# Two one-hot blocks in an expert layer, unread products in TensorE's waits, and three small edits in a quantised layer

## The chip, the cores and the metric

The kernel runs on one core of a Trainium2 chip. The metric is the time of one execution on the device in microseconds. Engines are named as the profile names them: PE (TensorE), PEld (its weight loads), DVE (VectorE), ACT (ScalarE), POOL (GpSimd), SP (SyncE, which issues most transfers).

## The reference

The input is x of 4 x 16 x 16 x 192 in f32: 1024 tokens of 192 numbers. Six layers follow one another, each added to its input; the change touches the last four.

```python
x = x + scan(_gn(x))            # state-space scan, four directions
x = x + neighbour(_gn(x))       # 7x7 neighbourhood attention
t = _to_tokens(x)
t = t + quantised(_ln_t(t))     # int8 attention and MLP
t = t + expert_m(_ln_t(t))      # 16 experts, top 2, and a shared one
t = t + attention(_ln_t(t))     # plain attention, one head
t = t + expert_g(_ln_t(t))      # 8 experts, top 2
```

The quantised layer rounds at every step: `fq(x, s) = clip(round(x / s), -128, 127) * s`.

```python
x_norm = fq(layernorm(x, g1, beta1), s_n1)
qkv = fq(x_norm @ fq(w_qkv).T + b_qkv, s_qkv)       # 12 heads of 16
attn = int_softmax(fq(q @ k.T * scale, s_attn))     # integer exponent, 2^(30-q)
x_attn = fq((attn @ v) @ fq(w_proj).T + b_proj, s_sv)
x = fq(x + x_attn, s_r1)
x_norm = fq(layernorm(x, g2, beta2), s_n2)
h = fq(gelu(x_norm @ fq(w_fc1).T + b_fc1), s_act)
h = fq(h @ fq(w_fc2).T + b_fc2, s_m2)
x = fq(x + h, s_r2)
```

The first expert layer:

```python
scores = softmax(xf @ gate_w.T)                     # 1024 x 16
topw, topi = top_k(scores, 2)
h = silu(xf @ w1[e].T) * (xf @ w3[e].T) * comb      # 512 wide, for the tokens of expert e
y = h @ w2[e].T ; z = silu(xf @ sw1.T) * (xf @ sw3.T) @ sw2.T
```

## The kernel before

Each layer is a block of its own; all engines finish one before the next begins. PE's time by layer: quantised 383 to 630 us, expert layer m 630 to 895, attention 895 to 960, last layer g 960 to 1104.

**Quantised layer** (`quantised_layer`). Tokens lie as 8 tiles of 128 (`X[:, t, :]`). The start normalises them (DVE), turns them on PE (f32 transposes, L1679), clips them on DVE into `nT` (bf16) and multiplies by `wqk` (`project`, L1696). Then 48 steps follow, one for each pair of image and head (4 images of 256 tokens, 12 heads). A head's chain is: PE scores (L1722), ACT rounds into `lt` (L1590), POOL clips (L1241), DVE takes the maximum (L1420) and subtracts it (`xi`, two L1425), POOL makes the quotient `qi` (L1251) and the power of two `e2` (L1268, 16-bit integers whose bits are read as bf16), PE forms the remainder in PSUM (L1742, L1743), ACT squares it (L1604), DVE multiplies by `e2` with a running sum (two L1443). `e2` has two buffers: before L1268 POOL waits until DVE is through with head h-2. Later PE turns the weights (L1734), DVE copies them (L1433), and the values are weighted. Each step of DVE's loop (index n) also carries side work: U of the first normalisation (L1476, tile n-12 for n = 12 to 19), the rescaled bias rows at n = 22 (L1478 to L1486), and after every image its `requantise`, on POOL for images 0 to 2 (L1214 to L1236).

The tail after the last head: DVE requantises image 3 (L1502 to L1507), statistics and N (L1362 to L1375), PE turns N (`turn_norm`, L1785), DVE clips into `nT` (L1389, L1391), PE makes 12 `up_product`s (L1823, two matmuls each: FT = 6 tiles for each half of the tokens), ACT the gelu (L1660), DVE rounds and clips it into `hi` (L1531, L1520, L1526), PE makes 4 `down_product`s. Each of these handles two token tiles, and begins a tile's sum with the bias row: `ones` (1 x 128) times `brow` (1 x 192), both f32 (L1837), then 6 bf16 matmuls (L1839). ACT evicts (L1667), DVE and ACT end the layer (L1544 to L1554, L1617).

**Expert layer m** (`expert_layer`, gated). After the normalisation `U` is split in f16 parts (`U16` is the high and the low part), PE turns it (L2429) and makes the logits, DVE picks two experts for each token and gives each token its places (slots) in the experts' lists. The plan is a list of blocks of 256 tokens: four shared blocks (0 to 3) and 23 routed ones. A block is `up_block` (40 matmuls, L2489 to L2493), silu on ACT (L2398), product with the gate on DVE (L2182), its high part on ACT (early blocks, L2413) or POOL (L2105), its low part on DVE (L2193), and `down_block` (L2511 to L2513). POOL writes all tokens to their slots in `scratch_x` in HBM by 16 indirect transfers (L2117); SP then reads each routed block's rows back (`load_rows`), after the last of the 16. PE turns the rows (six L2464) and ACT copies them into `xt` (L2375). Outputs go through `scratch_y` and are combined at the end. The layer g has the same form and already fetches its first three blocks by one-hot matmuls (`DIRECT` = 3): DVE compares a row of slot numbers with each token's seat (L2806), and PE multiplies the tokens with it.

Weights of a block come as f32 and are split by ACT (L2334, L2335, L2343) and DVE (L2167, L2169, L2175); `lo_ab` tells PE that a set's up weights are there. SP loads a set when DVE has left its stage.

Of the kernel before, what the change touches and what calls it, by code (L numbers as in the profile page):

```python
# [25 lines left out]
NB = 4  # L26
# [1096 lines left out]
def quantised_layer(nc, K, X, D):  # L1123

    with ExitStack() as stack:
# [25 lines left out]
        e2 = ctx.sb("q_e2", [P, 2, QT, L], I16)  # L1151
# [13 lines left out]
        brow = ctx.sb("q_brow", [1, C])  # L1165
        ones = ctx.sb("q_ones", [1, P])
# [9 lines left out]
        taken, late_part = S("taken"), S("late_part")  # L1176
# [23 lines left out]
        with nc.Block() as block:  # L1200
# [7 lines left out]
            def _(pool):  # L1208
                def requantise(at, p, part):
# [7 lines left out]
                    elif part == 1:  # L1217
                        pool.wait_ge(pool_steps, at + 2)
                        pool.tensor_scalar(f, f, -MAGIC, sc[:, S_SV:S_SV + 1], ALU.add, ALU.mult).then_inc(pool_steps, 1)
                        pool.wait_ge(pool_steps, at + 3)  # L1220
                        pool.tensor_tensor(f, f, batch(U, p), ALU.add).then_inc(pool_steps, 1)
# [37 lines left out]
                for h in range(HEADS):  # L1259
# [6 lines left out]
                    if h >= 2:  # L1266
                        pool.wait_ge(expd, (h - 1) * QT)
                    pool.tensor_scalar(e2[:, h % 2, :, :].rearrange("p q k -> p (q k)"), qi[:, h % 2, :], -128.0,  # L1268
                                       (127 + EXP_N + CENTRE) * 128.0, ALU.mult, ALU.add).then_inc(expo, 1)
                    if h % HG == HG - 1 and h < HEADS - NH:  # L1270
                        pool.wait_ge(scores, h + 1)
                        take(h // NH + 1, h % NH // HG)
                    if h >= TURN + 4 and h < TURN + 4 + 2 * NH and (h - TURN - 4) % NH < 3:
# [10 lines left out]
            def _(v):  # L1284
# [151 lines left out]
                def exponential(e):  # L1436
# [5 lines left out]
                    for q in range(QT):  # L1442
                        v.scalar_tensor_tensor(ex[:, e % NH, q, :], ps[:, 5 + e % 2, q * L:(q + 1) * L], k(K_CI), e2[:, e % 2, q, :].bitcast(BF16),  # L1443
# [17 lines left out]
                for n in range(STEPS):  # L1461
# [12 lines left out]
                    if 12 <= n < 12 + NT:  # L1474
                        t = n - 12
                        step(v.tensor_scalar(U[:, t, :], X[:, t, :], mv[:, t, 0:1], rs[:, 0, t:t + 1], ALU.subtract, ALU.mult))  # L1476
                    if n == 22:
# [7 lines left out]
                        step(v.tensor_scalar(brow[:, :], rows[0:1, 2, :], kf[0:1, K_PER:K_PER + 1], None, ALU.mult))  # L1485
# [24 lines left out]
                v.wait_ge(proj_read, 4)  # L1510
                requantise(3, S_SV, S_R1)
# [162 lines left out]
            def _(pe):  # L1674
                for half in range(NHALF):
# [7 lines left out]
                pe.wait_ge(K["q"]["quantised"], 20)  # L1683
# [24 lines left out]
                for n in range(6):  # L1708
                    project(n)
                pe.wait_ge(constants, 1)  # L1710
# [80 lines left out]
                for n in range(STEPS):  # L1791
# [1643 lines left out]
```

## Time and profile before

| | us |
|---|---|
| three runs, median | 1108.9 |
| three runs, lowest and highest | 1105.35 and 1115.82 |
| the profiled execution's own time | 1105.46 |
| its span on the core | 1103.7 |
| mean granted clock of PE in it | 0.817 of full speed |

The page shows the busy time of each engine and, in 40 slices, the clock that PE was granted. A stretch of the trace gives the same by windows. A timeline lists instructions in order with the idle time before them and what ended it. A group adds up all instructions of one line and shape. A "clock" of 1.00 is 2.4 GHz, of 0.50 it is 1.2 GHz; a number between is a stretch that holds both.

### The profile page before, as it was taken

What the parts mean: (1) busy time and instruction counts of PE and PEld (TensorE: products, weight loads), DVE (VectorE), ACT (ScalarE), POOL (GpSimd) and SP (SyncE); (2) the same over time, 40 slices, a digit from 0 to 9 for tenths busy, and PEclk for the clock granted to TensorE, in tenths of its full rate; (3) what the DMA queues carried; (4) which work ended last, traced back from release to release, by engine and by line L of the source; (5) the groups of instructions that cost most, each with busy time, mean ns of one, the idle gap of its engine ahead of it and who ended that gap; (6) DMA issues with size and microseconds to landing.
All of it is one profiled execution on the core that took longest, in us unless ns stands there. A gap on an engine that the chain in (4) does not pass through costs nothing. (4 is left out here: it accounts for less than half of the span.)

```text
span 1103.7 us, 17587 instructions
## 1 busy us (share of the span) xinstructions
PE 871.8 (79%) x6053; PEld 587.6 (53%) x6053; DVE 802.4 (73%) x1699; ACT 578.8 (52%) x977; POOL 424.3 (38%) x458
## 2 busy tenths in 40 slices
PE   8779999985999746667775564999999838658991
PEld 3333333333579722223452354999888715557991
DVE  6589999994675379998976673788888475583763
ACT  2755454421466445776764342677776146256760
POOL 0016666644046337668750005222222520034335
PEclk8889999996999865555556567999999958869996
DMA  8176666503000000000000093699994455102653
GB/s 254 42 205 171 170 168 161 152 20 86 1 2 2 11 2 1 1 1 1 1 1 1 13 230 100 166 269 267 257 270 126 136 155 154 52 26 84 209 206 89
DMA packets 61592, 117.59 MB, mean 107 GB/s; under 512 B 10240, under 2 KB 37312, under 8 KB 61504
## 3 DMA queue, kind: packets, MB, share of 16 engines
q1 hardware_dynamic: 58432, 110.18, 36.0%
q0 software_dynamic: 3072, 6.30, 1.9%
q8 instruction: 48, 0.79, 0.3%
q14 instruction: 40, 0.33, 0.1%
HBM read 90.79 MB, written 16.81 MB: 97 GB/s over the span
## 5 line engine op out<-in xcount | busy, mean ns | idle before, releaser
L459 POOL TENSOR_TENSOR hC<-hs,Cb 128x1024 f32<-128x1024 f32 x47 | 110.8, 2358 | 125.8 <-DVE hs L498 125.8
L498 DVE TENSOR_TENSOR_SCAN hs<-ps_l,dBu 128x1024 f32<-128x1024 f32 x48 | 109.9, 2290 | 2.8 <-ACT ps_l L590 1.2
L2105 POOL CAST m_h_hi<-m_h 128x512 f16<-128x512 f32 x54 | 49.0, 907 | 137.5 <-DVE m_h L2182 137.5
L658 PE MATMUL ps_l<-hC,selT 128*96 128x512 f32 x192 | 93.2, 609 | 1.5 <-POOL hC L459 1.5
L643 PE MATMUL ps_l<-du,sel 96*128 96x512 f32 x192 | 90.5, 593 | 1.4 <-DVE dBu L491 1.4
L590 ACT ACTIVATE ps_l<-d_sp,Am 128x1020 f32<-128x1020 f32 x48 | 53.5, 1115 | 71.5 <-DVE hs L498 71.3
L2511 PE MATMUL ps_m<-m_wd_hi,m_h_hi 128*128 128x192 f16 x248 | 62.9, 254 | 6.6 <-issue 3.5
L1742 PE MATMUL ps_l<-q_xi,identh 128*128 128x512 f16 x48 | 28.8, 599 | 48.5 <-POOL q_qi L1251 24.8
L2193 DVE TENSOR_TENSOR m_h_lo<-m_h,m_h_hi 128x512 f16<-128x512 f32 x62 | 42.9, 693 | 33.2 <-POOL m_h_hi L2105 30.1
L782 POOL TENSOR_TENSOR n_Pl<-n_PT,n_Ph 128x352 f16<-128x352 f32 x48 | 40.8, 853 | 65.6 <-ACT n_Ph L910 48.3
L2398 ACT ACTIVATE m_act<-ps_m 128x512 f32<-128x512 f32 x62 | 36.8, 593 | 52.8 <-PE ps_m L2493 48.6
L491 DVE TENSOR_TENSOR dBu<-ps_l,Bb 128x512 f32<-128x512 f32 x96 | 60.7, 674 | 4.0 <-PE ps_l L643 3.9
L2512 PE MATMUL ps_m<-m_wd_lo,m_h_hi 128*128 128x192 f16 x248 | 63.0, 254 | 0.0
L2513 PE MATMUL ps_m<-m_wd_hi,m_h_lo 128*128 128x192 f16 x248 | 63.0, 254 | 0.0
L643 PEld LDWEIGHTS ps_l<-du,sel 96*128 96x128 f32 x192 | 34.3, 188 | 51.2 <-DVE dBu L491 37.0
L658 PEld LDWEIGHTS ps_l<-hC,selT 128*96 128x96 f32 x192 | 27.4, 162 | 58.8 <-POOL hC L459 31.9
L2749 POOL DMA_INDIRECT scratch_x<-g_U,g_slot x16 | 19.3, 1208 | 96.9 <-DVE g_who L2867 89.8
L1599 ACT ACTIVATE q_pi<-q_ex,q_kf,q_fac 128x256 f16<-128x256 f32 x96 | 51.4, 589 | 0.8 <-PE ps_l L1734 0.8
L2489 PE MATMUL ps_m<-m_xt,m_wa_hi 128*128 128x256 f16 x184 | 50.4, 274 | 1.1
L2117 POOL DMA_INDIRECT scratch_x<-m_U,m_slot x16 | 17.3, 1080 | 87.4 <-DVE m_who L2276 77.9
L2182 DVE SCALAR_TENSOR_TENSOR m_h<-ps_m,m_act 128x512 f32<-128x512 f32 x62 | 42.5, 685 | 11.5 <-ACT m_act L2398 6.5
L2492 PE MATMUL ps_m<-m_xt,m_wb_hi 128*128 128x256 f16 x184 | 50.2, 273 | 0.0
(576 smaller groups left out, 2894.0 us busy)
## 6 DMA issues: line engine op xcount, KB each, us to landing
d_sp<-scan_d SPq DMA_DIRECT2D x48, 512.0 KB, 4.4
m_sta<-in_m_ua SPq DMA_DIRECT2D x25, 512.0 KB, 4.3
m_stb<-in_m_ub SPq DMA_DIRECT2D x50, 256.0 KB, 5.8
m_std<-in_m_dn SPq DMA_DIRECT2D x25, 384.0 KB, 6.7
gw_dn_in<-gw_dn SPq DMA_DIRECT2D x10, 576.0 KB, 3.3
scratch_x<-zero SPq DMA_DIRECT2D x1, 4416.0 KB, 21.1
m_xg<-scratch_x SPq DMA_DIRECT2D x23, 192.0 KB, 6.4
scratch_y<-m_o SPq DMA_DIRECT2D x23, 192.0 KB, 6.5
```

The source lines that it names most:

```text
L459: pool.tensor_tensor(hC[:, n % 2, :], hs[:, n % 2, :], Cb[:, which(n), :], ALU.mult).then_inc(weighted, 1)
L491: v.tensor_tensor(dBu[:, n % 2, half * BANK:(half + 1) * BANK], ps[:, 4 + half, :], Bb[:, which(n), half * BANK:(half + 1) * BANK], ALU.mu ...
L498: v.tensor_tensor_scan(hs[:, n % 2, ::step], dA(n)[:, ::step], dBu[:, n % 2, ::step], 0.0, ALU.mult, ALU.add).then_inc(scanned, 1)
L590: act.activation(dst[:, :, o:o + L - 1], d_sp[:, n % NSP, :].rearrange("p (b t) -> p b t", t=L)[:, :, o:o + L - 1], ACT.Exp, scale=Am[:, c ...
L643: pe.matmul(ps[:, 4 + half, :], sel[:, n % NG, :], du[:, n // NG, half * BANK:(half + 1) * BANK], start=True, stop=True).then_inc(du_bc, 1)
L658: mm = pe.matmul(ps[0:DI, 6 + half, :], selT[:, n % NG, :], hC[:, n % 2, half * BANK:(half + 1) * BANK], start=(n == STEPS), stop=(m == ST ...
L1599: act.activation(pi[:, p % 2, q, :], ex[:, p % NH, q, :], ACT.Identity, scale=fac[:, p % NH, q:q + 1], bias=kf[:, K_FLOOR:K_FLOOR + 1]).th ...
L2489: pe.matmul(out, wa_hi[a][:, col], x[:, 0, :], start=True, stop=False)
L2492: pe.matmul(out, wb_hi[a][:, col], x[:, 2, :], start=False, stop=False)
L2511: pe.matmul(out, h_hi[:, b % 2, f // 2, tok], wd_hi[a][:, col], start=(f == 0), stop=False)
L2512: pe.matmul(out, h_hi[:, b % 2, f // 2, tok], wd_lo[a][:, col], start=False, stop=False)
L2513: mm = pe.matmul(out, h_lo[:, b % 2, f // 2, tok], wd_hi[a][:, col], start=False, stop=(f == tiles - 1))
```

## The change

1. **Unread products.** `keep_busy(pe, K, out, n)` issues n matmuls of 96 rows by 512 columns in bf16 into a PSUM bank that nothing reads before it is written again. It stands at nine places: quantised layer, at the start (18; the wait for the quantised weights moves ahead of it), behind the first six `project` (14, behind a wait for `n_ready` 4), behind the last head's `shifted` (7), ahead of `turn_norm(6, 8)` (10, behind a wait for `proj_read`), ahead of `up_product(FT)` (10) and ahead of the last two `down_product` (5, behind a wait for all gelus); at the start of expert layer m (15), of the attention (11) and of the last layer (15).
2. **Quantised layer.** `e2` gets a third buffer. The eight U operations move from DVE (n = 12 to 19) to POOL (h = 12 to 19), with a negated mean `nmean` made by DVE at n = 11; waits `minus` and `unit` guard them. The bias row becomes three bf16 parts in three rows, `ones` three rows in bf16: DVE makes 9 small operations where there was one, PE one bf16 matmul of three rows where it had one f32 matmul of one row.
3. **Expert layer m.** `DIRECT` is 2: routed blocks 0 and 1 (plan blocks 4 and 5) take their tokens by one-hot matmuls (24 of 256 columns each) in place of reading rows from `scratch_x` and six transposes. DVE makes `seat` and the one-hot matrices, eight L2806-like operations of 128 x 256 for each block, in plan blocks 1 and 2. ACT makes the high parts for six blocks instead of four (`EARLY`). The first read of rows is for plan block 6.

```diff
+def keep_busy(pe, K, out, n):
+    w = K["q"]["wqk"]
+    for _ in range(n):
+        pe.matmul(out, w[:, 0:P], w[:, 0:BANK], start=True, stop=True)
...
-        e2 = ctx.sb("q_e2", [P, 2, QT, L], I16)
+        e2 = ctx.sb("q_e2", [P, 3, QT, L], I16)
...
-        brow = ctx.sb("q_brow", [1, C])
-        ones = ctx.sb("q_ones", [1, P])
+        brow = ctx.sb("q_brow", [3, C], BF16)
+        brest = ctx.sb("q_brest", [3, C])
+        bpart = ctx.sb("q_bpart", [3, 3, C], BF16)
+        nmean = ctx.sb("q_nmean", [P, NT])
+        ones = ctx.sb("q_ones", [3, P], BF16)
...
+                        pool.wait_ge(unit, NT)
                         pool.tensor_tensor(f, f, batch(U, p), ALU.add).then_inc(pool_steps, 1)
...
-                    if h >= 2:
-                        pool.wait_ge(expd, (h - 1) * QT)
-                    pool.tensor_scalar(e2[:, h % 2, :, :].rearrange("p q k -> p (q k)"), qi[:, h % 2, :], -128.0,
+                    if h >= 3:
+                        pool.wait_ge(expd, (h - 2) * QT)
+                    pool.tensor_scalar(e2[:, h % 3, :, :].rearrange("p q k -> p (q k)"), qi[:, h % 2, :], -128.0,
...
+                    if 12 <= h < 12 + NT:
+                        t = h - 12
+                        pool.wait_ge(minus, 1)
+                        pool.tensor_scalar(U[:, t, :], X[:, t, :], nmean[:, t:t + 1], rs[:, 0, t:t + 1], ALU.add, ALU.mult).then_inc(unit, 1)
...
-                    if 12 <= n < 12 + NT:
-                        t = n - 12
-                        step(v.tensor_scalar(U[:, t, :], X[:, t, :], mv[:, t, 0:1], rs[:, 0, t:t + 1], ALU.subtract, ALU.mult))
+                    if n == 11:
+                        v.tensor_scalar(nmean[:, :], mv[:, :, 0], -1.0, None, ALU.mult).then_inc(minus, 1)
...
-                        step(v.tensor_scalar(brow[:, :], rows[0:1, 2, :], kf[0:1, K_PER:K_PER + 1], None, ALU.mult))
+                        step(v.tensor_scalar(brest[:, :], rows[0:3, 2, :], kf[0:3, K_PER:K_PER + 1], None, ALU.mult))
+                        for part in range(3):
+                            step(v.tensor_copy(bpart[:, part, :], brest[:, :]))
+                            if part < 2:
+                                step(v.tensor_tensor(brest[:, :], brest[:, :], bpart[:, part, :], ALU.subtract))
+                        mine = lambda part: K["ident"][0:3, part:part + 1]
+                        step(v.tensor_scalar(brow[:, :], bpart[:, 0, :], mine(0), None, ALU.mult))
+                        for part in (1, 2):
+                            step(v.scalar_tensor_tensor(brow[:, :], bpart[:, part, :], mine(part), brow[:, :], ALU.mult, ALU.add))
...
+                pe.wait_ge(K["q"]["quantised"], 20)
+                keep_busy(pe, K, ps[:, 0, :], 18)
...
+                pe.wait_ge(n_ready, 4)
+                keep_busy(pe, K, ps[:, 4, :], 14)
                 pe.wait_ge(constants, 1)
...
+                pe.wait_ge(shifted, HEADS)
+                keep_busy(pe, K, ps[:, 0, :], 7)
                 turn_sums(NB - 1)
...
+                pe.wait_ge(proj_read, NB)
+                keep_busy(pe, K, ps[:, 7, :], 10)
                 turn_norm(6, 8)
-                for n in range(4, FF2 - 2):
+                for n in range(4, FT):
+                    up_product(n)
+                keep_busy(pe, K, ps[:, 7, :], 10)
+                for n in range(FT, FF2 - 2):
                     up_product(n)
                 for p in range(2):
                     down_product(p)
                     up_product(FF2 - 2 + p)
+                pe.wait_ge(gelu, FF2)
+                keep_busy(pe, K, ps[:, 0, :], 5)
                 for p in (2, 3):
                     down_product(p)
...
-    DIRECT = 0 if gated else 3
-    EARLY = (FIRST if gated else DIRECT) * PAIRS
+    DIRECT = 2 if gated else 3
+    EARLY = (FIRST + DIRECT) * PAIRS
...
+                step(v.scalar_tensor_tensor(seat[:], rank, 1.0, both[:], ALU.add, ALU.mult))
                 if not gated:
-                    step(v.scalar_tensor_tensor(seat[:], rank, 1.0, both[:], ALU.add, ALU.mult))
                     one_hot(0)
...
+                    if gated and 1 <= b <= DIRECT:
+                        one_hot(b - 1)
...
             def _(pe):
+                keep_busy(pe, K, ps[:, 7, :], 15)
```

The last line stands in expert layer m and in the last layer; the attention has the same with 11. What `one_hot` and `turn` do in the one-hot case:

```python
for t in range(NT):      # DVE, one_hot(n)
    v.tensor_scalar(hot[:, n % 2, t, :], slots1[:, :], seat[:, t, n:n + 1], None, ALU.is_equal)
for part in range(PARTS_X):      # PE, turn(b): PARTS_X = 3, NT = 8
    for t in range(NT):
        pe.matmul(out, U16[:, t, part * P:(part + 1) * P], hot[:, n % 2, t, :], start=(t == 0), stop=(t == NT - 1))
```

## Rows read from the trace of the kernel before

**Rows 1.** The page: PE's granted clock in 40 slices of the span (27.6 us each)

```profile
PEclk8889999996999865555556567999999958869996
```

**Rows 2.** Stretches (from:to, length, busy us of PE, PEld, DVE, ACT, POOL; clock, DMA, GB/s)

```profile
389.30:392.70 3.40, 2.94 (x14) 2.77 (x15) 3.12 (x15) 1.11 (x2) 0.00 (x0) 0.50 0.00 0
...
392.80:396.20 3.40, 2.05 (x11) 0.90 (x10) 3.08 (x15) 2.67 (x5) 0.00 (x0) 1.00 0.01 2
...
480.00:565.00 85.00, 61.90 (x333) 30.55 (x333) 79.03 (x245) 61.24 (x108) 61.92 (x98) 0.50 0.00 1
...
600.70:614.40 13.70, 13.31 (x44) 6.54 (x44) 6.64 (x21) 3.88 (x5) 0.00 (x0) 0.50 0.00 0
...
614.40:630.20 15.80, 8.14 (x33) 4.92 (x32) 12.02 (x30) 5.84 (x9) 0.00 (x0) 0.50 0.00 1
...
645.50:673.80 28.30, 25.09 (x224) 21.83 (x224) 20.21 (x69) 11.96 (x18) 9.27 (x8) 0.88 0.67 172
...
673.80:688.50 14.70, 0.02 (x1) 0.00 (x0) 2.08 (x3) 1.85 (x3) 8.02 (x9) 0.58 0.27 87
...
695.40:842.00 146.60, 145.58 (x1505) 132.59 (x1504) 121.58 (x150) 104.63 (x150) 39.62 (x42) 1.00 0.93 252
```

**Rows 3.** Groups of DVE, 400 to 572 us (count | busy, mean ns | idle before, releaser)

```profile
L1420 DVE TENSOR_REDUCE q_nm<-q_lt 128x2 f32<-128x512 f16 x48 | 32.6, 679 | 6.8 <-POOL q_lt L1241 6.3
...
L1476 DVE TENSOR_SCALAR q_U<-X,q_mv,q_rs 128x192 f32<-128x192 f32 x8 | 3.1, 393 | 0.0
...
L1485 DVE TENSOR_SCALAR q_brow<-q_rows,q_kf 1x192 f32<-1x192 f32 x1 | 0.3, 307 | 0.0
```

**Rows 4.** All 96 instructions of line 1425 by duration

```profile
L1425 DVE TENSOR_SCALAR q_xi<-q_lt,q_nm,q_kf x96: 333/394/778, 407.0 to 562.3; 128x256 f16<-128x256 f16 x96
```

**Rows 5.** Groups of POOL, 400 to 572 us

```profile
L1268 POOL TENSOR_SCALAR q_e<-q_qi 128x512 int16<-128x512 f16 x48 | 29.7, 618 | 12.4 <-DVE q_ex L1443 10.4
...
L1231 POOL TENSOR_SCALAR q_U<-q_pj,q_sc 128x384 f32<-128x384 f32 x2 | 1.2, 581 | 0.2
```

**Rows 6.** Timeline of PE at the quantised layer's start and tail, DVE's last rows

```profile
394.50 2.87 PE L1696 MATMUL ps_l<-q_nT,q_wqk 96*128 96x512 bf16 x12 [1.35 <-DVE q_nT L1330]
...
600.68 3.59 PE L1823 MATMUL ps_l<-q_nT,q_w 96*128 96x512 bf16 x8 [4.34 <-DVE q_nT L1391]
...
604.67 0.97 PE L1837 MATMUL ps_l<-q_brow,q_ones 1*128 1x192 f32 x2 [0.39 <-DVE q_hi L1526]
...
605.58 1.14 PE L1839 MATMUL ps_l<-q_w,q_hi 128*128 128x192 bf16 x6
...
629.63 0.56 DVE L1554 TENSOR_TENSOR X<-X,q_pj 128x384 f32<-128x384 f32 x1
```

**Rows 7.** Expert layer m: timelines of POOL, PE, DVE and ACT; SyncE's wait, 695 to 842

```profile
637.57 2.74 PE L2429 MATMUL ps_m<-identh,m_U 128*128 128x128 f16 x24 [12.36 <-ACT m_U L2353]
...
677.58 0.60 ACT L2398 ACTIVATE m_act<-ps_m 128x512 f32<-128x512 f32 x1 [2.41 <-DMA beta<-in_out_b]
...
683.52 0.96 POOL L2117 DMA_INDIRECT scratch_x<-m_U,m_slot  x1 [0.36 <-DMA scratch_x<-m_U,m_slot]
...
688.51 0.82 PE L2464 MATMUL ps_m<-identh,m_xg 128*128 128x128 f16 x6 [14.70 <-DMA m_xg<-scratch_x]
...
694.29 1.22 DVE L2167 SCALAR_TENSOR_TENSOR m_wa_lo<-m_sta,m_wa_hi 128x1024 f16<-128x1024 f32 x1
...
701.23 1.22 DVE L2167 SCALAR_TENSOR_TENSOR m_wa_lo<-m_sta,m_wa_hi 128x1024 f16<-128x1024 f32 x1
...
708.90 0.59 ACT L2398 ACTIVATE m_act<-ps_m 128x512 f32<-128x512 f32 x1
...
SPq L2032 <- DVE m_wd_lo L2175: 67.5, 19, 10.8
```

**Rows 8.** Last layer, group of DVE: its own one-hot instruction

```profile
L2806 DVE TENSOR_SCALAR g_hot<-g_slots,g_seat 128x128 f16<-128x128 f16 x48 | 8.6, 272 | 0.0
```

**Rows 9.** Timeline of PE at the start of the attention

```profile
899.19 3.88 PE L1866 MATMUL ps_l<-ident,a_U 128*96 128x128 f32 x16 [16.84 <-DVE a_U L178]
```

More of the change, by code:

```diff
@@ L1175, in quantised_layer @@
             S("proj"), S("evac"), S("q_part"), S("qk_ready"), S("v_proj"), S("v_steps"), S("v_ready"))
-        taken, late_part = S("taken"), S("late_part")
+        taken, late_part, minus, unit = S("taken"), S("late_part"), S("minus"), S("unit")
         scores, shifted, clipped, negmax, diff, quot, rest, expo, square, expd, factor = (
@@ L1442, in exponential @@
                     for q in range(QT):
-                        v.scalar_tensor_tensor(ex[:, e % NH, q, :], ps[:, 5 + e % 2, q * L:(q + 1) * L], k(K_CI), e2[:, e % 2, q, :].bitcast(BF16),
+                        v.scalar_tensor_tensor(ex[:, e % NH, q, :], ps[:, 5 + e % 2, q * L:(q + 1) * L], k(K_CI), e2[:, e % 3, q, :].bitcast(BF16),
                                                ALU.add, ALU.mult, accum_out=sums[:, e % NH, q:q + 1]).then_inc(expd, 1)
@@ L1510, in _ @@
                 v.wait_ge(proj_read, 4)
+                v.wait_ge(unit, NT)
                 requantise(3, S_SV, S_R1)
@@ L1682, in _ @@
                                 mm.then_inc(turned_n, 1)
-                pe.wait_ge(K["q"]["quantised"], 20)
                 def project(n):
@@ L1953, in expert_layer @@
         first = ctx.sb(f"{pre}_first", [P, routed])
-        slots1 = None if gated else ctx.sb(f"{pre}_slots1", [P, BS], F16)
+        slots1 = ctx.sb(f"{pre}_slots1", [P, BS], F16)
         seat = ctx.sb(f"{pre}_seat", [P, NT, routed])
-        hot = None if gated else ctx.sb(f"{pre}_hot", [P, 2, NT, BS], F16)
+        hot = ctx.sb(f"{pre}_hot", [P, 2, NT, BS], F16)
         lg = ctx.sb(f"{pre}_lg", [P, NT, routed])
@@ L2018, in expert_layer @@
         counts = ps[:, 5, 0:routed] if gated else ps[:, 6, NR:NR + routed]
-        LOADS = 64 if gated else 96
+        LOADS = 80 if gated else 96
         WD = 4
@@ L2069, in _ @@
                     sync.dma_start(bo[:, :], D[f"{pre}_bo"]).then_inc(loaded, 16)
-                    sync.dma_start(slots1[:, :], D["slots1"]).then_inc(loaded, 16)
+                sync.dma_start(slots1[:, :], D["slots1"]).then_inc(loaded, 16)
                 for w in range(NST):
@@ L2967, in _ @@
             def _(pe):
+                keep_busy(pe, K, ps[:, 7, :], 15)
                 for q in range(4):
@@ L3206, in _ @@
             def _(pe):
+                keep_busy(pe, K, ps[:, 7, :], 11)
                 tr.tensor(pe, use - 1, ln, use, U, ps, K["ident"])
```

## The prediction

> **What bounds the kernel now.** I read the page first, for PE's clock by slices [rows 1]: nearly full through the first two layers, half from about 390 to 650 us (the quantised layer and the start of m), and it dips again near the start of the last two layers. Then the windows by stage [rows 2], to see which engine is full in each.
>
> - In the heads of the quantised layer DVE is busy 79.03 of 85 us; PE, at 1.2 GHz, 61.90. DVE sets the pace. Of its idle time, 6.8 us over all 48 heads, 6.3 is for POOL's clip [rows 3]. A faster PE alone buys little here.
> - In the tail, from 600.7 to 614.4, PE is busy 13.31 of 13.70 us at 1.2 GHz [rows 2]: its own time is the path.
> - In layer m, after the four shared blocks, PE stands for 14.70 us until the routed rows are read back; the last of the 16 indirect transfers starts at 683.52, and only then can the read begin [rows 2, 7]. Nothing but this order holds PE.
> - In the run of routed blocks DVE's first split of a weight set starts every 701.23 - 694.29 = 6.94 us. SyncE waits 67.5 us for DVE to free a stage, so transfers keep up, though with a DMA share of 0.93 the room is small [rows 2, 7]. Blocks after the stall keep their pace, so what is won at the stall stays won.
>
> **The change part by part**, against the profiled execution's own 1105.5 us (span 1103.7, and 1.8 around it). The median of the runs lies 3.4 above it.
>
> *Heads.* U off DVE: eight times 0.393 [rows 3], -3.1. `nmean`, one operation of 128 x 8: below the 0.307 of L1485, +0.2. The bias row is eight more operations of 192 columns at 0.307 [rows 3], +2.5; I take +2.8, since four have two inputs. On POOL a U operation has half the columns of L1231 (0.581), so 0.3 to 0.6 [rows 5]; POOL is idle for 23 of 85 us [rows 2], 0.7 a head, and that hides it; without the cover it costs 8 x 0.45 = 3.6. Third `e2` buffer: POOL's wait of 10.4 us for L1443 [rows 5] goes. To the loop it is worth at most the 6.3 us that DVE waits for L1241 [rows 3], and nothing if POOL then waits longer for `xi` instead. I take -2.0, a third, because POOL is late only in the first heads and where it requantises. Together -2.1, range -5 to +3.
>
> A POOL operation that overlaps with `xi` (L1425) seems to lengthen it: 0.333 at the shortest, 0.394 in the median, 0.778 at the longest [rows 4]. Earlier POOL work shifts which ones are hit; within the range above.
>
> The Trainium skill, page "SBUF — State Buffer", section "Who interferes with whom", says that a VectorE instruction in a 2-port mode and a GpSimd one exclude each other for the whole instruction. By it an `xi` that meets POOL's clip would take its own time plus all of POOL's; the longest in the trace is short of that, and most are far below. The rule speaks against more work on POOL; as a mechanism of this kernel it is rival 4.
>
> *Clock at the start.* Twelve 512-column products took 2.87 us at 2.4 GHz and eight 3.59 at 1.2 [rows 6], 0.24 and 0.45 each. So the 18 at the start are 4.0 to 8 us, the 14 ahead of the heads 3.1 to 6. But the stretch between is DVE's (3.12 and 3.08 busy of 3.40 [rows 2]): a faster PE wins 0.2 there, and 18 cold products can end up to 1.1 late. In the loop a warm PE would be busy only about a third to half of the time (61.90 of 85 at half clock [rows 2]), and I expect it back at 1.2 GHz.
>
> The clock was full from 392.8, behind a stretch at 1.2 GHz with only f32 transposes [rows 2]. The Trainium skill, page "TensorE: Matmul & The Clock Gate", section "Part 4: PE-mode transpose", says that full speed does not engage for transposes. The trace disagrees; by the page the products would be needed everywhere, by the trace they are worth less where transposes already fill the stretch.
>
> *Tail.* A token tile of a down product spends 0.97 us on L1837's two f32 passes and 1.14 on six of L1839, 0.19 each [rows 6]. One bf16 pass in place of the two costs 0.19, so each of eight tiles saves about 0.8. Four lie ahead of the last up product: -3.2. Four lie behind it; there DVE is busy 12.02 of 15.80 us [rows 2] up to its last operation at 629.63 [rows 6], so at most 3.8 can go, and the first wait of DVE lies ahead of these products: -2.5. Together -5.7 at 1.2 GHz. The clock: 7 products behind the last head and 10 + 10 around the turns of N lie in waits such as the 4.34 us ahead of L1823 at 600.68 [rows 6]. If they hold 2.4 GHz, the path gives up to -1.9 before 587 and -3.6 from 600.7 on, where 13.31 us of PE would halve but gelu and rounding then set the pace. If not, ten products are 4.5 us in a wait of 4.34, and with those of the other places up to 2.7 late. I take half of what can be won, -2.8. Tail -8.5, range -4.5 to -11.5.
>
> *Layer m.* Start: 15 products (3.6 or 6.8 us) fit in PE's wait of 12.36 [rows 7]; the turns of U come partly at full clock: -0.5 (0 to -1.5). One-hot blocks: DVE gets `seat` (0.3) and sixteen operations of 128 x 256. The nearest row has half the columns, 0.272 [rows 8], so 0.25 to 0.5 each, which includes some overlap with the next; I take 0.25, 2.0 us a block. DVE is busy 20.21 of 28.30 us among the shared blocks [rows 2]; that hides more than half of the 4.3, 1.6 reach PE, and the last shared up block ends at 675.4 instead of 673.8 (without cover 678). From there PE does not wait. In the run of blocks 6.94 us hold 40 up matmuls of 256 columns, 24 down ones of 192 and six transposes, 15,600 columns, so 0.11 us for 256 and 0.083 for 192: up 4.4, down 2.0, and 24 one-hot matmuls 2.6 in place of six transposes in 0.82 [rows 7]. One-hot, down of block 2, up of 4, one-hot, down of 3, up of 5: to 693.4; with down of 4 and the transposes the up of block 6 starts at 696.9. Before, block 6's first silu is at 708.90 [rows 7]; its up began 20 matmuls, 2.2 us, earlier, at 706.7. That is -9.8, and -10.6 with the read of rows (landed by 688.5) out of the way. Against it, ACT shows gaps such as 2.41 us at 677.58 [rows 7] while the scatter runs, which the stall hid: +2. So -8.6, range -5 to -12.
>
> *Attention and last layer.* The 16 transposes at the attention's start take 3.88 us [rows 9] at 1.2 GHz, 2.0 at 2.4; the 11 products lie in a wait of 16.84 [rows 9] and may end 0.5 late. -1.5 (0 to -3). In the last layer the stretch behind the products is mostly DVE's: -0.3.
>
> Sum: -0.2 - 2.1 - 8.5 - 0.5 - 8.6 - 1.5 - 0.3 = -21.7: 1083.8 against the profiled execution, 1087.2 against the median. I say 1086.
>
> **The rivals.**
>
> 1. *The clock stays up in the heads too.* The 14 products start the loop at full clock. For it: PE has work for 61.90 of 85 us [rows 2]. Against: that halves at 2.4 GHz, and DVE sets the pace. At most -5 more: 1081.
> 2. *The products hold the clock nowhere.* Waits outlast them. Then 2.8 + 0.5 + 1.5 + 0.5 of gain goes and about 2 comes on: 1093.
> 3. *The one-hot blocks only move the stall.* ACT makes high parts for six blocks and DVE the one-hots while the scatter disturbs both, or the next splits are late. Then m gives 3 instead of 8.6: 1092. With rival 2, 1099.
> 4. *Slower: POOL blocks `xi`.* If POOL's operations hold the port for whole instructions, each of two `xi` a head goes from 0.39 toward 0.78 [rows 4]. From 0.45 us a head on average (48 x 0.45 = 21.6) the whole gain is gone; at 0.7 it is 1120. For it: the spread of rows 4. Against: the same overlaps exist before, and the mean is near the short end.
>
> **How the numbers follow.** Chances: forecast 0.48, rival 1 0.10, rival 2 0.20, rival 3 0.13, rivals 2 and 3 together 0.05, rival 4 0.04. The range 1073 to 1100 holds rivals 1 to 3 and, downward, the far ends of tail and m with rival 1. A measurement of this kernel can tell about 1%, 11 us, from no change. Faster by more (below 1098): the first four nearly whole, 0.86. Within 1%: rivals 2 and 3 together, and what falls short in the others, 0.10. Slower, rival 4: 0.04.
>
> **What would show it.** Right: L1837 eight times at about 0.2 us; no idle of PE before plan block 4; the up of block 6 about 10 us earlier after its layer's start than before; clock 1.00 over the products of the tail; no POOL wait for L1443. Wrong: heads that take longer; PE waits for ACT or DVE in blocks 4 to 6; a period above 6.94; unread products that end after what they stand beside.

## The result and the profile after

| | before | changed |
|---|---|---|
| median of four runs | 1107.5 us | 1088.65 us (1087.9 to 1097.0) |
| span of the profiled execution | 1103.7 us | 1086.8 us |
| mean granted clock in it | 0.817 | 0.845 |

The ratio is 0.9863 with a 95% interval of 0.982 to 0.9905, so the kernel is 1.4% faster. I had said 1086 us.

The page of the changed kernel, busy time and PE's clock by slices:

```profile
PE 895.2 (82%) x6186; PEld 595.0 (55%) x6186; DVE 805.4 (74%) x1717; ACT 580.5 (53%) x983; POOL 423.3 (39%) x462
...
PEclk8889999997999875556658579999999888868995
```

Against [rows 1] the half-speed slices of the quantised layer are still there. The slice of the attention's start went from 5 to 8; the 6 near the end stays. The stretches that answer to [rows 2], same columns:

```profile
476.00:560.00 84.00, 55.51 (x329) 28.32 (x328) 79.84 (x247) 59.72 (x105) 60.43 (x96) 0.60 0.00 1
595.20:606.10 10.90, 9.87 (x40) 4.72 (x40) 6.52 (x21) 3.68 (x5) 0.00 (x0) 0.54 0.00 0
606.10:619.70 13.60, 7.08 (x33) 3.61 (x33) 12.01 (x30) 5.84 (x9) 0.00 (x0) 0.63 0.00 1
633.70:662.50 28.80, 25.38 (x214) 22.00 (x215) 23.13 (x85) 11.95 (x18) 8.50 (x8) 0.82 0.61 176
662.50:685.20 22.70, 21.72 (x219) 19.74 (x217) 15.18 (x21) 14.09 (x23) 9.88 (x9) 1.00 0.38 117
685.20:831.80 146.60, 145.31 (x1491) 131.85 (x1492) 119.69 (x147) 103.45 (x149) 39.61 (x42) 1.00 0.87 244
```

Heads: DVE is still the full engine. Tail: 10.9 us where there were 13.7, at nearly the same clock (0.54 against 0.50). Layer m: the 14.70 us in which PE did nothing are gone; from 662.5 to 685.2 it is busy 21.72 of 22.70 us. The long run of blocks is what it was, DMA share 0.87.

Because single executions differ by several us in places that the change does not touch, I measured each stage from the same instructions in every trace. Each column below is one execution, not a mean. "Heads" is from the first score matmul to the maximum of head 48, "tail" from there to the quantised layer's last operation, "m start" from there to the first up matmul, "m blocks 0 to 5" to the first up matmul of block 6. "Last layer, blocks" is from its first to its last down product. Lengths in us:

| stage | before | changed | changed, 2nd execution | 3rd | no products | one-hot only | f32 bias | bias late |
|---|---|---|---|---|---|---|---|---|
| layers ahead | 389.8 | 386.7 | 387.0 | 390.2 | 390.3 | 386.6 | 388.8 | 386.2 |
| start of the quantised layer | 14.1 | 14.1 | 14.1 | 14.1 | 14.0 | 14.1 | 14.1 | 14.1 |
| heads | 157.4 | 155.4 | 155.4 | 157.0 | 157.0 | 157.2 | 153.1 | 153.4 |
| tail | 68.9 | 63.6 | 61.6 | 61.4 | 62.7 | 69.0 | 68.9 | 60.3 |
| m start | 15.4 | 14.0 | 13.9 | 15.1 | 14.8 | 14.8 | 14.8 | 15.1 |
| m blocks 0 to 5 | 60.8 | 51.5 | 51.7 | 50.5 | 50.0 | 50.8 | 51.1 | 50.1 |
| rest of m, to the attention's turns | 192.8 | 192.6 | 192.9 | 193.1 | 194.0 | 193.6 | 193.3 | 193.0 |
| attention: turns, first 8 projections | 10.3 | 6.9 | 6.5 | 6.8 | 10.3 | 7.8 | 6.7 | 6.7 |
| rest of the attention | 49.8 | 49.4 | 50.8 | 47.8 | 49.9 | 49.9 | 48.6 | 48.0 |
| last layer, to its first down | 30.9 | 30.8 | 30.8 | 30.1 | 30.1 | 30.1 | 30.0 | 30.1 |
| last layer, blocks | 86.5 | 94.5 | 86.8 | 86.9 | 88.8 | 86.9 | 89.0 | 88.2 |
| combination | 27.0 | 27.3 | 27.6 | 27.4 | 27.0 | 27.4 | 27.0 | 27.1 |
| span | 1103.7 | 1086.8 | 1079.1 | 1080.3 | 1088.8 | 1088.0 | 1085.4 | 1072.4 |

The columns come from several chips. "No products", "one-hot only" and "f32 bias" ran on chip 1 (as did e3), the 2nd execution on chip 7 (as did e6, e7 and e8), the 3rd and "bias late" on chip 6 (as did e9). The chip of the first two columns is not known.

The first two columns account for the -16.9 of the span: -3.1 ahead of the change, -2.0 heads, -5.4 tail, -1.4 m start, -9.3 blocks 0 to 5, -0.2 rest of m, -3.8 attention, and +8.3 in the last layer. The last is the surprise: there the change only puts 15 products ahead of the layer.

### The profile page after: what moved, and what is told of

The parts are those of the page before. It is cut to its first block and busy times, and to the rows that moved or that the text cites. A ratio compares the mean times of both kernels' runs of the same rounds, so it can differ in the third digit from the quotient of the medians.

```text
span 1086.8 us, 17877 instructions
## 1 busy us (share of the span) xinstructions
PE 895.2 (82%) x6186; PEld 595.0 (55%) x6186; DVE 805.4 (74%) x1717; ACT 580.5 (53%) x983; POOL 423.3 (39%) x462
## 5 line engine op out<-in xcount | busy, mean ns | idle before, releaser
L2140 POOL CAST m_h_hi<-m_h 128x512 f16<-128x512 f32 x50 | 45.2, 904 | 127.4 <-DVE m_h L2217 127.4
L1768 PE MATMUL ps_l<-q_xi,identh 128*128 128x512 f16 x48 | 27.6, 574 | 50.0 <-POOL q_qi L1262 26.1
L665 PEld LDWEIGHTS ps_l<-hC,selT 128*96 128x96 f32 x192 | 27.4, 162 | 58.8 <-POOL hC L466 31.9
L2839 DVE TENSOR_TENSOR g_h_lo<-g_act,g_h_hi 128x384 f16<-128x384 f32 x46 | 26.1, 570 | 38.0 <-ACT g_h_hi L2997 23.7
L2787 POOL DMA_INDIRECT scratch_x<-g_U,g_slot x16 | 17.0, 1061 | 92.0 <-DVE g_who L2905 86.6
L1613 ACT ACTIVATE q_lt<-ps_l,q_kf 128x512 f16<-128x512 f32 x48 | 37.1, 775 | 25.7 <-DVE q_xi L1440 17.6
```

The source lines that it names most:

```text
L665: mm = pe.matmul(ps[0:DI, 6 + half, :], selT[:, n % NG, :], hC[:, n % 2, half * BANK:(half + 1) * BANK], start=(n == STEPS), stop=(m == ST ...
L2140: pool.tensor_copy(h_hi[:, b % 2, q, :], src).then_inc(h_high, 1)
```

## The experiments

The time of the kernel before differs from chip to chip (medians of 1100 to 1107 us), so ratios to it on the same chip are given, and the stages decide.

**No unread products** (e1).

```diff
 def keep_busy(pe, K, out, n):
-    for _ in range(n):
+    for _ in range(0):
```

> The changed kernel without any of the unread products (all waits that stand with them stay). Theory A, the products pay by the clock: the attention from its first transposes to its end is about 3.5 us longer than in the changed kernel, the quantised tail from the last head to the layer's end 1 to 3 us longer, the starts of layer m and of the quantised layer under 1; total 5 to 7 us above the changed kernel's 1088, unless the last layer gets its 8 us back. Theory B, the products hold the clock nowhere: all segments within 0.5 us of the changed kernel. Theory C on the last layer, whose scatter stretch is 8 us longer in the changed kernel (engines stand there with no releaser but 'issue' and 'remote'): if the 15 products ahead of it shift how PE's instructions lie and so cause it, that stretch is about 8 us shorter here, and the total is near 1086.

Ratio 0.9875 (0.9837 to 0.9912). The attention's start is 10.31 us again, as before (10.25), against 6.9 with the products: 3.4 by the clock. That counts from the first turn. The products let this turn start 0.83 us after DVE's first U tile, and without them it starts after 0.06, so some 2.6 of the 3.4 are left. The window, columns as above, is at half speed for most of its length:

```profile
600.77:610.42 9.65, 9.26 (x40) 4.24 (x40) 6.66 (x21) 3.89 (x5) 0.00 (x0) 0.60 0.01 2
...
882.70:893.00 10.30, 9.62 (x25) 5.04 (x26) 8.74 (x15) 7.47 (x10) 0.00 (x0) 0.56 1.00 243
```

The first row is the tail from up product 6 (counted from 0) to the last: 9.65 us at a clock of 0.60 without products, 10.93 at 0.54 with them in the first execution. The whole tail is 62.7 us, within the 61.4 to 63.6 of the changed kernel's three executions, so the 2.8 us I had booked are not there; e6 looks closer. Theory A holds for the attention alone. In the total the products can't be told from nothing: the intervals of e1 and of the changed kernel overlap, and beside e3 on the same chip, which lacks only the last layer's products, e1's median is 5.0 us higher (1089.3 and 1084.3). Theory C got a first hint, 88.8 us of blocks in the last layer in place of 94.5, but see e3 to e5.

**One-hot blocks alone** (e2): the kernel before with part 3.

```diff
-    DIRECT = 0 if gated else 3
-    EARLY = (FIRST if gated else DIRECT) * PAIRS
+    DIRECT = 2 if gated else 3
+    EARLY = (FIRST + DIRECT) * PAIRS
...
+                    if gated and 1 <= b <= DIRECT:
+                        one_hot(b - 1)
```

> The kernel before with part 3 alone (two one-hot blocks in layer m). Theory A, the stall was all that counted: layer m from its first transposes to the end of its last down product is 9 to 11 us shorter than before, total 1097 to 1099 against 1107.5. Theory B, part of the gain of m in the changed kernel came from the clock held by the products: m is only 5 to 8 us shorter. If the last layer's scatter stretch is also longer here, its 8 us do not come from the products.

Ratio 0.9902 (0.9875 to 0.993). Blocks 0 to 5 take 50.8 us against 60.8, and all other stages of the quantised layer and the last are within 0.8 us of before. The one-hot blocks give their 9 to 10 us alone; no unread products are needed. This is the largest part of the gain, and the total agrees: 1090.2 against 1100.2 on this chip. The attention's start was short here too (7.8) without products: its first eight projections ran at full clock, in 3.51 us. So of three executions without products at that place two paid the half clock and one mostly did not; the 3.4 is what the products give where the clock is not up by itself.

**Last layer without its products** (e3).

```diff
             def _(pe):
-                keep_busy(pe, K, ps[:, 7, :], 15)
```

> The changed kernel without the 15 products at the start of the last layer, all others stay. Theory C, those products cause the longer scatter stretch there (by where PE's later instructions lie): from the first one-hot to the last down product about 8 us shorter, total about 1081. Rival, the stretch is longer for another reason (what the layers before leave, or chance from execution to execution): the last layer takes what it takes in the changed kernel, within 1 us, total 1088 to 1089.

Ratio 0.9844 (0.9811 to 0.9877). Blocks of the last layer 88.2 us, 6 less, as theory C asked. But e4, which has the 15 products, gave 89.0, so the products are not the cause.

**Bias as one f32 row** (e4).

```diff
-        brow = ctx.sb("q_brow", [3, C], BF16)
+        brow = ctx.sb("q_brow", [1, C])
...
-                        step(v.tensor_scalar(brest[:, :], rows[0:3, 2, :], kf[0:3, K_PER:K_PER + 1], None, ALU.mult))
+                        step(v.tensor_scalar(brow[:, :], rows[0:1, 2, :], kf[0:1, K_PER:K_PER + 1], None, ALU.mult))
```

> The changed kernel with the bias row of the second MLP matmul again as one f32 row. By the prediction's step: up to the end of the last up product 3.2 us more, behind it 2.5 more, in the heads 2.5 less (eight small operations of DVE), so the tail is 5.7 longer at 1.2 GHz and the kernel about 3 slower, 1091 to 1092. Rival, the clock of the tail takes part of it: at 2.4 GHz the f32 passes cost half, the tail is only 3 longer and the kernel within 1 us of the changed one.

Ratio 0.9851 (0.9803 to 0.99). The windows of heads, of up products 6 to 11, and from there to the layer's end:

```profile
402.93:556.05 153.12, 106.46 (x528) 46.26 (x528) 143.44 (x428) 108.34 (x180) 118.27 (x192) 0.54 0.00 1
595.02:608.78 13.76, 13.37 (x44) 6.55 (x44) 6.65 (x21) 3.88 (x5) 0.00 (x0) 0.50 0.00 0
608.78:624.97 16.19, 10.34 (x37) 5.51 (x37) 12.01 (x30) 5.84 (x9) 0.00 (x0) 0.50 0.00 1
```

With the f32 row they are 13.76 and 16.19, against 10.93 and 13.61 in the first execution of the changed kernel, the one whose clock there (0.54) is nearest: 2.8 and 2.6 us, where the steps had 3.2 and 2.5. Of the 2.6, 0.4 belongs to the five unread products, since the same stretch took 15.8 us before. Even with all the tail's products, the clock here was 0.50 in both windows. The heads are 2.3 us shorter than in the first execution and 3.0 shorter than the mean of the changed heads (see e7 and e8; 2.8 booked). The net of the bias row is thus -2.4 to -3 us, and its cost sits in the loop where DVE is full. The totals agree less exactly: e4's median is 2.0 us above e3's on the same chip, where I had expected 3, and at 1086.3 it is not the 1091 to 1092 that I had named.

**The changed kernel again** (e5 and e11).

> The changed kernel once more, nothing altered. It tells what is chance in one profiled execution. Theory A, the long scatter stretch of the last layer (94.5 us from its first down product to its last, 86.5 before) belongs to the changed kernel: 93 to 96 again. Theory B, it is chance (86.9 to 89.0 in the four other kernels): 86 to 90, and the sum of the unchanged layers up to the quantised layer's first transposes (386.6 to 390.6 so far) moves by some us too.

> The changed kernel beside the two others on the same chip. The last layer from first to last down product 85 to 95 us, the longer the closer its 16 indirect transfers lie (22 us of scatter went with 94.5, 27 us with 86.8); all else within 1 us of the earlier looks but for the clock in the heads.

Ratios 0.9895 (0.9844 to 0.9946) and 0.9835 (0.9805 to 0.9865). Blocks of the last layer 86.8 and 86.9 us, spans 1079.1 and 1080.3. The same program gave 94.5, 86.8 and 86.9, so the 94.5 does not belong to the kernel; the second and third ran on chips 7 and 6 at other times, so that it is chance within one chip is not shown. Two warnings on the columns: e5's profiled execution (1080.9 us) is the fastest of its ten runs, which reach 1101.9 with a median of 1093.3. And the third execution is not "within 1 us" of the others as I had expected: heads +1.6, layers ahead +3.2, rest of the attention -3.0 against the second.

Where the 94.5 lay: PE's and ACT's waits around the scatter, 951 to 983 us of the first execution (engine, instruction, releaser: us in total, times, longest):

```profile
PEld ps_g L3063 <- issue: 7.8, 4, 4.5
ACT g_xt L2970 <- remote: 6.5, 1, 6.5
ACT g_o L2977 <- remote: 5.2, 1, 5.2
PE ps_g L3063 <- issue: 4.7, 2, 3.9
```

and 950 to 985 us of the second:

```profile
PEld ps_g L3063 <- issue: 5.3, 3, 2.7
ACT g_xt L2970 <- remote: 4.6, 2, 3.1
...
PE ps_g L3063 <- issue: 2.5, 1, 2.5
```

"issue" and "remote" are waits for nothing that the profile shows. They lie where the 16 indirect transfers run. Over the scatter, PEld's "issue" adds up to 11.7 us in the first execution (scatter 22.4 us long), 4.9 in the second (26.6 long), 1.1 in the third (26.1), and 10.3 in e7 (23.2 long, blocks 92.6). The two shortest scatters go with the two longest stretches of blocks; all others have 26.1 to 29.4 us of scatter and 84.9 to 89.0 of blocks.

**Tail without its products** (e6).

```diff
                 pe.wait_ge(shifted, HEADS)
-                keep_busy(pe, K, ps[:, 0, :], 7)
...
-                pe.wait_ge(proj_read, NB)
-                keep_busy(pe, K, ps[:, 7, :], 10)
...
-                keep_busy(pe, K, ps[:, 7, :], 10)
...
-                pe.wait_ge(gelu, FF2)
-                keep_busy(pe, K, ps[:, 0, :], 5)
```

> The changed kernel without the products of the quantised tail (7, 10, 10 and 5); the waits beside them go too, all other products stay. Theory A, they keep 2.4 GHz over the tail as I forecast: from the last head to the layer's end 2 to 4 us longer than with them. Theory B, they mostly find the clock anyway where DVE sets the pace: within 1 us. Theory C, cold they end late: without them the stretch from up product 6 to the last is about 1 us shorter (9.65 without any products against 10.93), and the total 1 us lower.

Ratio 0.9806 (0.9724 to 0.9887). The tail takes 63.7 us, and e1 without products there 62.7; with them and the bf16 row it is 63.6, 61.6, 61.4, 62.1 (e3), 62.9 (e7), 63.1 (e8) and 62.0 (e9). The means are 63.2 and 62.4: the products are worth some 0.8 us, within what single executions differ by. Theory B. Theory C failed: from up product 6 to the last it is 11.10 us here, longer than with the products. The same stretch in e6, in the third execution and in e10:

```profile
595.66:606.76 11.10, 10.70 (x40) 4.95 (x40) 6.65 (x21) 3.89 (x5) 0.00 (x0) 0.50 0.00 0
```

```profile
599.39:609.05 9.66, 7.74 (x40) 3.89 (x40) 6.56 (x21) 3.56 (x5) 0.00 (x0) 0.78 0.00 0
```

```profile
592.63:600.52 7.89, 5.96 (x40) 3.17 (x40) 6.57 (x21) 3.56 (x5) 0.00 (x0) 1.00 0.00 0
```

Of eight executions with the bf16 row and the products, six have a clock of 0.76 to 0.78 in it and take 9.7 to 10.0 us; the first execution of the changed kernel (0.54, 10.93) was the exception on one side and e10 on the other. So the products do hold part of the clock, against 0.50 and 0.60 without them, but little of it reaches the end of the layer. What e6's trace showed besides is the same kind of wait in layer m, at block 4, now that no stall hides it:

```profile
ACT m_act L2431 <- DMA xT<-in_xT: 7.1, 1, 7.1
DVE X L2233 <- remote: 6.7, 1, 6.7
...
PEld ps_m L2525 <- issue: 2.0, 3, 1.0
```

(The named transfer, the load of the input, had long been done.) Blocks 0 to 5 took 56.5 us here, 5 more than in the others.

**Two e2 buffers** (e7) and **U on DVE** (e8).

```diff
-                    if h >= 3:
-                        pool.wait_ge(expd, (h - 2) * QT)
+                    if h >= 2:
+                        pool.wait_ge(expd, (h - 1) * QT)
```

> The changed kernel with two e2 buffers again. By the prediction's step the heads become 2.0 us longer (155.4 to 157.4) and POOL's wait for L1443's successor is back at about 10 us. Rival: POOL only waits elsewhere, the heads stay within 0.7 us.

```diff
-                    if 12 <= h < 12 + NT:
-                        t = h - 12
-                        pool.wait_ge(minus, 1)
-                        pool.tensor_scalar(U[:, t, :], X[:, t, :], nmean[:, t:t + 1], rs[:, 0, t:t + 1], ALU.add, ALU.mult).then_inc(unit, 1)
...
-                    if n == 11:
-                        v.tensor_scalar(nmean[:, :], mv[:, :, 0], -1.0, None, ALU.mult).then_inc(minus, 1)
+                    if 12 <= n < 12 + NT:
+                        t = n - 12
+                        step(v.tensor_scalar(U[:, t, :], X[:, t, :], mv[:, t, 0:1], rs[:, 0, t:t + 1], ALU.subtract, ALU.mult))
```

> The changed kernel with the eight U operations back on DVE. By the prediction's step the heads become 2.9 us longer (155.4 to 158.3). Rival: on POOL they delay the clips and with them DVE's maxima, so the heads change by less than 1 us.

Heads 157.3 with two buffers and 159.1 with U on DVE, each from one execution. What to set them against matters: the changed heads took 155.4, 155.4, 157.0, 156.5 (e3), 155.9 (e6), 155.8 (e9) and 157.0 (e1, without products), mean 156.1, and were longest where their granted clock was 0.51 and shortest at 0.54 and 0.57. Against the mean, U on DVE costs 3.0 us (booked 2.9), clear of that spread. Two buffers cost 1.2 (booked 2.0), only 0.3 above the longest of the seven: the size is not shown by the heads, and the case for the third buffer is the wait that it removes. The waits of POOL, first e7, then the changed kernel, then its U on POOL:

```profile
L1279 POOL TENSOR_SCALAR q_e<-q_qi 128x512 int16<-128x512 f16 x48 | 29.8, 622 | 9.6 <-DVE q_ex L1458 7.1
```

```profile
L1279 POOL TENSOR_SCALAR q_e<-q_qi 128x512 int16<-128x512 f16 x48 | 29.7, 619 | 4.0
...
L1287 POOL TENSOR_SCALAR q_U<-X,q_nmean,q_rs 128x192 f32<-128x192 f32 x8 | 4.2, 526 | 0.0
```

The wait for DVE is gone. A U operation costs POOL 0.526, within the 0.3 to 0.6, and hides. Back on DVE it took 0.570 rather than the 0.393 of before: six of the eight take 0.63 to 0.64 and end 0.11 us after a POOL L1278 (`e2`) that they meet, where before it was one, at 0.54:

```profile
L1486 DVE TENSOR_SCALAR q_U<-X,q_mv,q_rs 128x192 f32<-128x192 f32 x8 | 4.6, 570 | 0.0
```

**One indirect transfer at a time in the last layer** (e9).

```diff
-                    if n >= 2:
-                        pool.wait_ge(scattered[n % 2], 16 * (n // 2))
+                    if n >= 1:
+                        pool.wait_ge(scattered[(n - 1) % 2], 16 * ((n - 1) // 2 + 1))
```

> The changed kernel with the last layer's 16 indirect transfers one at a time: each waits for the one before it instead of for the one before that. Theory D, engines stand without a releaser ('issue', 'remote') because indirect transfers packed closely hold up what the engines' instructions come by: then these waits inside the scatter shrink (PEld under 2 us against 4.9 and 11.7 in two looks at the changed kernel), while the scatter itself takes 30 to 50 us instead of 22 to 29, and the rows for the fourth block may come late by up to 15 us, which is a wait for g_xg, not 'issue'. Rival, the waits have nothing to do with the transfers' density: PEld's share stays at 4 to 12 us.

The scatter takes 45.4 us, and inside it no engine has a wait "issue" or "remote" left. Instead PE waits for the rows 25 us, where I had said up to 15, and the kernel is at 1100.7 (1082.9 with two at a time on the same chip):

```profile
PE ps_g L3041 <- DMA g_xg<-scratch_x: 25.0, 1, 25.0
```

This looks like theory D, but it does not show it. e9 ran on chip 6. There the changed kernel with two transfers at a time (e11) has 1.1 us of such waits on PEld and none on PE, ACT or DVE inside the same scatter, so there was next to nothing to take away. The last section sets the executions side by side.

**Bias late** (e10), a version meant to be kept: the nine bias operations stand behind the last head instead of at n = 22, `down_product(0)` waits for two signals of `scaled2`, and the last layer has no products. These are two changes at once; e3 gave no sign that the second matters.

```diff
+                step(v.tensor_scalar(brest[:, :], rows[0:3, 2, :], kf[0:3, K_PER:K_PER + 1], None, ALU.mult))
...
+                v.scalar_tensor_tensor(brow[:, :], bpart[:, 2, :], mine(2), brow[:, :], ALU.mult, ALU.add).then_inc(scaled2, 1)
+
                 read_projection(3)
```

> Aimed at a better version: the changed kernel with the nine bias operations moved out of the heads to behind the last head, where DVE waits 4 us for the projection's product, and without the products of the last layer. Theory, they cost 2.25 us in the heads (155.4 against 153.1 without them) and nothing where they go: heads 153 to 154, from the last head to the layer's end as before (62 to 63.5), total 2 us below the changed kernel of the same call. Rival, that stretch is not free (the requantisation behind it starts late): it grows by 1 to 2 us and nothing is won.

Ratio 0.9787 (0.9754 to 0.9819), median 1077.8 us beside 1082.9 for the changed kernel on the same chip. The heads are 153.4, and in the tail DVE (start, us, operation) does the nine in its wait:

```profile
576.00 0.30 DVE L1522 TENSOR_SCALAR q_brest<-q_rows,q_kf 3x192 f32<-3x192 f32 x1
...
578.68 0.41 DVE L1530 SCALAR_TENSOR_TENSOR q_brow<-q_bpart,ident,q_brow 3x192 bf16<-3x192 bf16 x1
579.48 0.62 DVE L1395 SCALAR_TENSOR_TENSOR q_pj<-ps_l,q_kf,q_rows 128x384 f32<-128x384 f32 x1 [0.39 <-PE ps_l L1798]
```

PE's product still comes 0.39 us after them, so they cost nothing there. This version beats both kernels, the changed one by 5 us where 2 were expected. Of the profiled executions' difference, 3.6 us lie in the heads and 1.1 in the tail, where the clock over up products 6 to 11 was 1.00 here and 0.78 in e11; 4.0 lie ahead of the change, by chance.

## Why the prediction was right, point by point

**The total.** -21.7 was forecast, -16.9 measured in the first profiled execution. The difference is the +8.3 of the last layer and the -3.1 ahead of the change, neither of which the same program showed again in full; the stages that the change touches give -22.1. That this meets -21.7 so closely is luck: the tail gave 3.1 too little, while the attention gave 2.3, the start of m 0.9 and the blocks of m 0.7 more than booked. The median of the first runs was right to within 3 us.

**Heads, -2.1: measured -2.0** in the first execution, -1.3 from before to the mean of seven. Against that mean the parts are U -3.0 (forecast -2.9), third buffer -1.2 (-2.0, the least certain), bias +3.0 (+2.8); they add up to -1.2. The lengthening of `xi` did come: all 96, shortest, median and longest as in [rows 4],

```profile
L1440 DVE TENSOR_SCALAR q_xi<-q_lt,q_nm,q_kf x96: 333/368/780, 403.6 to 557.1; 128x256 f16<-128x256 f16 x96
```

and the group of them and of the maximum (as in [rows 3]),

```profile
L1440 DVE TENSOR_SCALAR q_xi<-q_lt,q_nm,q_kf 128x256 f16<-128x256 f16 x96 | 42.5, 485 | 1.7
L1435 DVE TENSOR_REDUCE q_nm<-q_lt 128x2 f32<-128x512 f16 x48 | 32.4, 675 | 4.8 <-POOL q_lt L1252 4.7
```

The mean went from 0.468 to 0.485, and with U on DVE it is 0.462: 1.6 us of DVE in all against before, far from rival 4's 20. The wait for the clip fell from 6.3 to 4.7. The longest `xi`, 0.780, is short of its own 0.333 plus the whole of a clip's 0.614.

The prediction made too little of this overlap. In the first execution 47 of the 96 `xi` take more than 0.4 us, and each of the 47 ends 0.077 to 0.080 us after the end of a POOL operation; before it was 48 of 48. Two `xi` in a row, and the POOL operations beside them:

```profile
483.83 1.25 DVE L1440 TENSOR_SCALAR q_xi<-q_lt,q_nm,q_kf 128x256 f16<-128x256 f16 x2
483.91 0.40 POOL L1247 COPY q_qkb<-q_qk 128x256 bf16<-128x256 bf16 x1
484.39 0.61 POOL L1252 TENSOR_SCALAR q_lt<-q_lt 128x512 f16<-128x512 f16 x1
```

POOL is through at 485.00 and the second `xi` at 485.08. On such an overlap the Trainium skill, page "SBUF — State Buffer", section "Who interferes with whom", has the one that comes second wait until the other's instruction is done. The trace agrees, with the 0.08 us on top. My prediction had read the page as the sum of both times, and from `xi` being shorter than that had taken the trace to speak against it; what `xi` waits for is what is left of POOL's operation. (Which of the two came first can't be read off the starts: the `xi` of 0.78 us start some 0.09 us before the POOL operation that they outlast by 0.08.) Over its shortest time of 0.333 the mean `xi` lost 0.135 us before and 0.152 after, 12.9 and 14.5 us in the heads, where DVE sets the pace. So rival 4's mechanism was there all along, and the change added only 1.6 us to it.

**Tail, -8.5: measured -5.4** (-7.4 in the two later executions). The step that failed is a size: the -2.8 for the clock, worth some 0.8 by e1 and e6. PE in the tail of the first execution (start, us, instruction; L70 is the unread product, L1865 the bias row, L1867 the rest of the sum):

```profile
590.03 2.32 PE L70 MATMUL ps_l<-q_wqk 96*128 96x512 bf16 x10
595.15 2.80 PE L1851 MATMUL ps_l<-q_nT,q_w 96*128 96x512 bf16 x8 [2.80 <-DVE q_nT L1406]
598.98 0.31 PE L1865 MATMUL ps_l<-q_brow,q_ones 3*128 3x192 bf16 x1 [1.02 <-DVE q_hi L1549]
599.22 1.14 PE L1867 MATMUL ps_l<-q_w,q_hi 128*128 128x192 bf16 x6
...
606.96 2.31 PE L70 MATMUL ps_l<-q_wqk 96*128 96x512 bf16 x5 [0.87 <-ACT q_hf L1683]
```

The ten products ran at 2.4 GHz, 2.3 us, and after them PE still waited 2.80: they fill less than half of the wait, and the clock was at 1.2 GHz from 596.0, at the beginning of the work it was to help. Where it was up (e10, 7.89 us for up products 6 to 11), it helped. From 606.1 on, all versions with the bf16 row take 13.5 to 13.6 us whatever the clock, as DVE's 12.01 of 13.60 sets the end. I had counted half of a gain that lay mostly behind DVE. The bias row itself was right: -5.4 of -5.7 with the products beside it, -4.9 without them (11.10 and 13.53 us in e6, 13.76 and 15.75 before). Its matmul took 0.25 to 0.34 us, not the 0.2 I had named.

**Layer m, -8.6: measured -9.3** (-10.8 to -9.1 in the other kernels of the table that have the one-hot blocks). Prices, as groups:

```profile
L2288 DVE TENSOR_SCALAR m_hot<-m_slots,m_seat 128x256 f16<-128x256 f16 x16 | 3.3, 284 | 0.0
...
L2492 PE MATMUL ps_m<-m_hot,m_U 128*128 128x256 f16 x48 | 5.6, 272 | 0.0
```

3.3 us of DVE for both blocks (4.0 booked), 2.8 us of PE for each (2.6). The read of rows was no longer waited for. The 2 us I held back for gaps during the scatter came in one execution only: 0 in most, 5 in e6. Start of m: -1.4 against before, but -0.6 of that is there without products as well, and with them single executions spread from 13.3 to 15.1 us, so the 0.5 booked for them can't be confirmed. In the working, the chain from 693.4 with the down of block 4 (2.0) and the transposes (0.8) ends at 696.2, not 696.9: the forecast for m was 0.7 short by its own terms.

**Attention, -1.5: measured -3.8**, of which 3.4 in its first ten us. The products run up to the layer's first turns, at 1.2 GHz, 0.44 each:

```profile
873.16 4.85 PE L70 MATMUL ps_l<-q_wqk 96*128 96x512 bf16 x11 [10.99 <-PEq L2059]
877.81 2.64 PE L1901 MATMUL ps_l<-ident,a_U 128*96 128x128 f32 x16
```

The turns take 2.64 in place of 3.88 [rows 9] and the f32 projections behind them start at 2.4 GHz; I had counted the turns (1.9) less some lateness, and not the projections (3.51 for eight in place of 5.7). The lateness, booked at 0.5, was 0.8: a sign I had named as wrong, products that end after what they stand beside, did come here, and the gain outweighed it. The projections can have the clock without the products too (e2).

**Quantised start, last layer: nothing, as forecast** (14.0 to 14.1 us in all; 29.98 to 30.9, with and without products). At the quantised start the 18 products only moved the full clock: it was granted from 384.4 to 391.1 in the first execution and was down from 391.3, where it had been up from 392.8 to 399.5 before.

**Rivals.** 1 (clock up in the heads) did not come: 0.60 in the window, by single short rises. 2 was nearly true for the tail (some of the clock held, 0.8 us gained), false for the attention. 3 was false but for e6's trace. 4 exists, and what the change added to it is small.

## What to carry to other kernels

Taking a dependency out of the way (rows made by matmul instead of a trip through HBM) kept its full worth alone and in company, 8 to 11 us in all executions but e6's (4.3). Unread products paid clearly only where they ran up to the moment at which PE-bound work began, at the attention, and there in two of three comparisons; in the tail, where a wait outlasts them or another engine sets the pace behind them, what they gave (0.8 us) is not clear of the spread between executions. New side work belongs where its engine waits, not in the loop in which it is full: moving nine small operations took 2 to 3.6 us from the heads. And a part of 1 or 2 us is not measured by one execution against one other: the same heads differed by 1.6 us.

## What the runs showed of the hardware

**VectorE and GpSimd.** A f16 `tensor_scalar` of VectorE (128 x 256, 0.333 us at its shortest) that meets a GpSimd operation ends 0.08 us after it: 48 of the 48 longer than 0.4 us before, 47 of 47 in the changed kernel, 40 of 40 in e8. It takes up to 0.780 us.

**Waits without a releaser while 16 indirect transfers run.** Inside the last layer's scatter (us in total of "issue" and "remote"):

| executions | chip | PEld | ACT | DVE | scatter | blocks of the last layer |
|---|---|---|---|---|---|---|
| before, changed | not known | 4.5, 11.7 | 4.7, 8.8 | 5.5, 0 | 26.5, 22.4 | 86.5, 94.5 |
| e5, e6, e7, e8 | 7 | 4.9, 4.5, 10.3, 3.9 | 5.7, 3.7, 8.2, 4.2 | 1.6, 1.5, 0, 2.9 | 26.6, 29.4, 23.2, 27.1 | 86.8, 88.6, 92.6, 84.9 |
| e1, e2, e3, e4 | 1 | 1.1, 1.1, 1.3, 1.0 | 0 | 0 | 27.4, 26.1, 28.6, 27.4 | 88.8, 86.9, 88.2, 89.0 |
| e10, e11 | 6 | 1.2, 1.1 | 0 | 0 | 27.4, 26.1 | 88.2, 86.9 |
| e9, one at a time | 6 | 0 | 0 | 0 | 45.4 | 108.1 |

The waits sort by chip, or by when it was measured, and not by kernel: every execution of the first two rows has them on ACT, none of the others has. In layer m's scatter it is the same, but for one wait of PEld of 3.4 to 3.9 us that every execution has (e6: a single wait of 7.1 us on ACT and one of 6.7 on DVE). Whether the chip itself or something that ran beside it at that time makes them is open. e9 lies among the quiet ones, so whether one transfer at a time would remove the waits is open as well; what it shows is its price, 45.4 us instead of 22 to 29. Nor are the waits the whole length of the stretch: e8 has several and the shortest blocks of all.
